# Edge sums of the first two layers of a four-layer graph network: partial sums gathered by PSUM strips of neighbouring node tiles

## The reference

```python
# layer 0 (attention, 4 heads)
h = x @ W;  e = leaky(a_src[src] + a_dst[dst]);  alpha = softmax of e over the edges of each dst
x1 = layernorm(x + prelu(segment_sum(alpha * h[src], dst) + bias))
# layer 1
msg = relu(x1[src] + edge_attr)
z = x1 + segment_sum(msg, dst);  then two dense layers and a norm
# layer 2: segment_sum(support[src] * edge_weight, dst)
# layer 3: attention over the edges with 8 heads, then a feed-forward part
```

## Time and profile before

| | us |
|---|---|
| median of the runs | 6502.33 |
| span of the profiled execution | 6898.0 |
| PE busy | 4580.7 (66%) |
| DVE busy | 4207.2 (61%) |
| ACT busy | 2924.2 (42%) |
| POOL busy | 4137.4 (60%) |

### The profile page before, as it was taken

The page is one execution under the profiler, slowest core; times in us unless marked ns, Lnnn a source line. Parts: engine busy times, 40 slices in busy tenths (PEclk is TensorE's granted clock), DMA queues, the critical chain, the costliest instruction groups (busy, mean ns, idle before and its releaser), DMA issues. The chain is left out here.

```text
span 6898.0 us, 99476 instructions
## 1 busy us (share of the span) xinstructions
PE 4580.7 (66%) x17620; PEld 3435.1 (50%) x17621; DVE 4207.2 (61%) x10350; ACT 2924.2 (42%) x8245; POOL 4137.4 (60%) x3730
## 2 busy tenths in 40 slices
PE   7366666660455555586777777775567777777799
PEld 5234344430233333375666666664455555555688
DVE  4366666677455555684444444445589988988554
ACT  0133233335233333252222222222278988888543
POOL 1666666632666666326888888883367777777110
PEclk9566666675676766797766777777888988988899
DMA  6344444424555555316888888886556656666110
GB/s 202 106 109 110 110 109 109 110 75 153 161 180 176 173 172 176 119 63 119 132 131 131 132 131 131 132 131 183 178 161 187 187 177 185 188 180 185 41 33 28
DMA packets 704342, 947.56 MB, mean 137 GB/s; under 512 B 99439, under 2 KB 560847, under 8 KB 704176
## 3 DMA queue, kind: packets, MB, share of 16 engines
q0 software_dynamic: 277808, 587.53, 37.0%
q1 hardware_dynamic: 406928, 338.53, 17.1%
q10 hardware_dynamic: 19440, 19.79, 0.8%
HBM read 756.06 MB, written 189.40 MB: 137 GB/s over the span
## 5 line engine op out<-in xcount | busy, mean ns | idle before, releaser
L1712 POOL DMA_INDIRECT gcn<-c_update,c_target x832 | 1300.0, 1563 | 271.5 <-issue 231.9
L1308 PE MATMUL psum<-g_rows,g_onehot 128*128 x1664 | 635.5, 532 | 745.8 <-issue 240.9
L664 POOL DMA_INDIRECT e_rows<-hrow,e_idx x832 | 822.3, 988 | 463.2 <-issue 236.9
L2078 POOL DMA_INDIRECT s_rows<-kv,s_idx x832 | 798.3, 960 | 372.0 <-issue 224.5
L1200 POOL DMA_INDIRECT g_rows<-x,g_idx x784 | 765.2, 976 | 414.7 <-issue 222.2
L1308 PEld LDWEIGHTS psum<-g_rows,g_onehot 128*128 128x128 f32 x1664 | 396.7, 260 | 984.5 <-issue 928.2
L727 PE MATMUL psum<-e_rows,e_onehot 128*128 128x265 f32 x1664 | 668.9, 559 | 275.0 <-issue 112.2
L2181 PE MATMUL psum<-queries_sums,s_spread 128*128 x1664 | 518.3, 466 | 249.4 <-issue 148.4
L727 PEld LDWEIGHTS psum<-e_rows,e_onehot 128*128 128x128 f32 x1664 | 403.6, 266 | 478.4 <-DVE acc L821 191.3
L1276 DVE TENSOR_TENSOR acc<-acc,psum 128x256 f32 x832 | 349.4, 420 | 439.6 <-issue 189.1
L1664 PE MATMUL psum<-support,c_mix 128*128 x1664 | 610.1, 531 | 0.0
(11 more groups left out here) (360 smaller groups left out, 9315.4 us busy)
## 6 DMA issues: line engine op xcount, KB each, us to landing
g_attr<-in_edge_attr SPq DMA_DIRECT2D x196, 512.0 KB
c_srow<-rows_src SPq DMA_DIRECT2D x208, 256.0 KB
e_drow<-rows_dloc SPq DMA_DIRECT2D x208, 128.0 KB
c_feat<-in_edge_feat SPq DMA_DIRECT2D x832, 32.0 KB
s_drow<-rows_dloc SPq DMA_DIRECT2D x208, 128.0 KB
n_sums<-gcn SPq DMA_DIRECT2D x100, 256.0 KB
e_rows<-hrow,e_idx POOLq DMA_INDIRECT x832
edge_rows<-c_edge_rows SPq DMA_DIRECT2D x208, 64.0 KB
```

Source lines behind the costliest of these rows:

```text
L664: pool.indirect_dma_start(rows[u][:, s, 0:D + H], None, k.hrow, bass.IndirectOffsetOnAxis(ap=idx[u][:, s:s + 1], axis=0)).then_inc(gathere ...
L1308: pe.matmul(k.psum[:, s, 0:D], onehot[q % 2][:, s, :], rows[:, bass.ds(m[q % 2 * GROUP + s], 1), :].rearrange("p o d -> p (o d)"), start=T ...
L1712: pool.indirect_dma_start(k.gcn[a], bass.IndirectOffsetOnAxis(ap=target[q][:, a:a + 1], axis=0), update[q][:, a, :], None, compute_op=ALU. ...
L2078: pool.indirect_dma_start(rows[at.u][:, st, 0:2 * D], None, k.kv, bass.IndirectOffsetOnAxis(ap=idx[at.u][:, st:st + 1], axis=0)).then_inc( ...
```

## The change

In each of the two layers the sums of several steps are gathered in PSUM before VectorE adds them.

*Layer 1.* A group has a strip of four neighbouring node tiles in PSUM (two banks; two strips take turns). The strip begins at the node tile of the group's first step (`base_at`, at most NT - 4); `part_at` holds for each step its place in the two strips. TensorE first writes zeros over the two banks (one-row bfloat16 matmuls of 512 columns), then adds the four steps into the places that the table names, and ends the two accumulations by two matmuls of 8 columns. VectorE adds the whole strip, 4 x 256 columns, in one instruction. TensorE waits once per group for the strip to be free (two groups back), POOL and `mark` count groups.

*Layer 0.* Two steps share a strip of two tiles, in two banks; two strips. The first step starts the first bank, a matmul of zeros starts the second, the second step goes to the bank that `second_part` names, and two matmuls of 8 columns end both. VectorE adds 2 x 265 columns per pair, and its order in a round is now: first pair of the group before, `weigh`, second pair, `mark`. TensorE reads two entries of `second_part` into registers per group.

Both layers get a few more small VectorE instructions ahead of their loops, to make the tables.

```diff
@@ gat_edges
-                        pool.wait_ge(summed, n * SB + (q + 1) * GROUP)
+                        pool.wait_ge(summed, n * PB + (q + 1) * 2)
...
             def add_up(n, u, q):
+                second = load_indices(nc, pe, second_part, n * PB + 2 * q, 2, 3)
                 pe.wait_ge(weighed, n * GB + q + 1)
                 pe.wait_ge(half_weighed, n * GB + q + 1)
                 pe.wait_ge(onehot_ready, n * GB + q + 1 + 1)
-                for s in range(GROUP):
-                    pe.wait_ge(added, n * NADD + q * GROUP + s + (3 if q else 1))
-                    pe.matmul(k.psum[:, s, 0:W], onehot[q % 2][:, s, :], rows[u][:, q * GROUP + s, :],
-                              start=True, stop=True).then_inc(summed, 1)
+                for h in range(2):
+                    pe.wait_ge(added, n * NADD + 2 * q + h + (3 if q else 1))
+                    here, beyond = 2 * h, 2 * h + 1
+                    pe.matmul(k.psum[:, beyond, 0:W], k.ones16[:], zero16[:], start=True, stop=False)
+                    pe.matmul(k.psum[:, here, 0:W], onehot[q % 2][:, 2 * h, :], rows[u][:, q * GROUP + 2 * h, :],
+                              start=True, stop=False)
+                    pe.matmul(k.psum[:, bass.ds(second[h], 1), 0:W].rearrange("p o w -> p (o w)"),
+                              onehot[q % 2][:, 2 * h + 1, :], rows[u][:, q * GROUP + 2 * h + 1, :],
+                              start=False, stop=False)
+                    pe.matmul(k.psum[:, here, 0:8], k.ones16[:], zero16[:, 0:8], start=False, stop=True)
+                    pe.matmul(k.psum[:, beyond, 0:8], k.ones16[:], zero16[:, 0:8], start=False, stop=True
+                              ).then_inc(summed, 1)
...
-            def add_group(n, q, js):
-                for s in range(GROUP):
-                    st = q * GROUP + s
-                    dve.wait_ge(summed, n * SB + st + 1 + 2 * SB)
-                    dve.wait_ge(added, n * NADD + 2 + st + GROUP)
-                    at = k.acc[:, bass.ds(js[st % 16], 1), :].rearrange("p o w -> p (o w)")
-                    dve.tensor_tensor(at, at, k.psum[:, s, 0:W], ALU.add).then_inc(added, 1)
+            def add_pair(n, q, h, js):
+                p = 2 * q + h
+                dve.wait_ge(summed, n * PB + p + 1 + 2 * PB)
+                dve.wait_ge(added, n * NADD + 2 + p + 2)
+                to = k.acc[:, bass.ds(js[p % 8], 2), :]
+                dve.tensor_tensor(to, to, k.psum[:, 2 * h:2 * h + 2, 0:W], ALU.add).then_inc(added, 1)
...
                         if not start:
-                            weigh(n - 1, 1 - u, q)
...
                             if q > 0:
-                                add_group(n - 1, q - 1, js)
+                                add_pair(n - 1, q - 1, 0, js)
+                            weigh(n - 1, 1 - u, q)
+                            if q > 0:
+                                add_pair(n - 1, q - 1, 1, js)
@@ gin_edges
+            by_group = lambda t: t[:].rearrange("o (g s) -> o g s", s=GROUP)
+            ch.tick(dve.memset(zero16[:], 0.0))
+            ch.then(dve.tensor_scalar(by_group(base_at), by_group(k.step_j)[:, :, 0:1].to_broadcast([1, GROUPS, GROUP]),
+                                      float(NT - GROUP), None, ALU.min))
+            ch.then(dve.tensor_tensor(part_at[:], k.step_j[:], base_at[:], ALU.subtract))
+            odd = part_at[:].rearrange("o (g b s) -> o g b s", b=2, s=GROUP)[:, :, 1, :]
+            dve.tensor_scalar(odd, odd, float(GROUP), None, ALU.add).then_inc(slots_ready, 1)
...
-            def step_group(at, j):
-                for s in range(GROUP):
-                    st = at.g * GROUP + s
-                    dve.wait_ge(summed, st + 1 + R)
-                    dve.wait_ge(stepped, st + GROUP)
-                    to = k.acc[:, bass.ds(j[s], 1), :].rearrange("p o w -> p (o w)")
-                    dve.tensor_tensor(to, to, k.psum[:, s, 0:D], ALU.add).then_inc(stepped, 1)
+            def sum_group(at, j):
+                dve.wait_ge(summed, at.g + 1 + 2)
+                dve.wait_ge(stepped, at.g + 2)
+                to = k.acc[:, bass.ds(j, GROUP), :]
+                dve.tensor_tensor(to, to, parts[:, at.q % 2 * GROUP:at.q % 2 * GROUP + GROUP, :], ALU.add
+                                  ).then_inc(stepped, 1)
...
+                        to = load_indices(nc, pe, part_at, at.g * GROUP, 2 * GROUP, 2 * GROUP - 1)
+                    pe.wait_ge(stepped, at.g + 1)
+                    banks = [k.psum[:, 2 * (q % 2) + n, :] for n in range(2)]
+                    for bank in banks:
+                        pe.matmul(bank, k.ones16[:], zero16[:], start=True, stop=False)
                     if at.has_tiles:
                         pe.wait_ge(msg_ready, at.g + 1 + RING)
                     pe.wait_ge(onehot_ready, at.g + 1 + 2)
                     for s in range(GROUP):
-                        pe.wait_ge(stepped, at.g * GROUP + s + 1)
-                        pe.matmul(k.psum[:, s, 0:D], onehot[q % 2][:, s, :],
-                                  rows[:, bass.ds(m[q % 2 * GROUP + s], 1), :].rearrange("p o d -> p (o d)"),
-                                  start=True, stop=True).then_inc(summed, 1)
+                        st = q % 2 * GROUP + s
+                        pe.matmul(parts[:, bass.ds(to[st], 1), :].rearrange("p o d -> p (o d)"), onehot[q % 2][:, s, :],
+                                  rows[:, bass.ds(m[st], 1), :].rearrange("p o d -> p (o d)"), start=False, stop=False)
+                    for bank in banks:
+                        ins = pe.matmul(bank[:, 0:8], k.ones16[:], zero16[:, 0:8], start=False, stop=True)
+                    ins.then_inc(summed, 1)
```

More of the change, by code:

```diff
@@ L588, in gat_edges @@
     T = SB + 1
-    NADD = SB + 2
+    PB = SB // 2
+    NADD = PB + 2
     SETUP = 5
@@ L614, in gat_edges @@
         scale = sb("e0_scale", [P, H])
+        first_tile, second_part = (sb(f"e0_{n}", [1, STEPS // 2], I32) for n in ("first_tile", "second_part"))
+        zero16 = sb("e0_zero16", [1, W], BF16)
         LOOK, WEIGHT, TURN, BACK = 4, 5, 6, 7
@@ L626, in gat_edges @@
                  "summed", "added", "chain", "cleared", "half_cleared"))
+        pairs_ready = sem("e0_pairs_ready")
         block = ctx.enter_context(nc.Block())
@@ L704, in _ @@
         def _(pe):
-            pe.sem_inc(summed, 2 * SB)
+            pe.wait_ge(pairs_ready, 4)
+            pe.sem_inc(summed, 2 * PB)
             pe.sem_inc(looked_up, 2)
@@ L770, in _ @@
             dve.sem_inc(spread_ready, RING)
-            dve.sem_inc(added, GROUP)
+            dve.sem_inc(added, 2)
             dve.sem_inc(onehot_ready, 1)
@@ L779, in _ @@
             assert setup.n == SETUP
+            of_pair = lambda a: k.step_j[:].rearrange("o (p a) -> o a p", a=2)[:, a, :]
+            dve.tensor_copy(first_tile[:], of_pair(0)).then_inc(pairs_ready, 1)
+            dve.tensor_tensor(second_part[:], of_pair(1), of_pair(0), ALU.subtract).then_inc(pairs_ready, 1)
+            dve.memset(zero16[:], 0.0).then_inc(pairs_ready, 1)
+            dve.wait_ge(pairs_ready, 3)
+            odd = second_part[:].rearrange("o (p a) -> o a p", a=2)[:, 1, :]
+            dve.tensor_scalar(odd, odd, 2.0, None, ALU.add).then_inc(pairs_ready, 1)
+            dve.wait_ge(pairs_ready, 4)
             dve.wait_ge(half_cleared, 1)
@@ L794, in mark @@
             def mark(n, q):
-                wait_if_any(dve, summed, n * SB + (q - 1) * GROUP + 2 * SB)
+                wait_if_any(dve, summed, n * PB + (q - 1) * 2 + 2 * PB)
                 one_hot(dve, k, onehot[q % 2], n * GB + q).then_inc(onehot_ready, 1)
@@ L808, in rescale @@
                 at = k.acc[:, bass.ds(j, 1), :].rearrange("p o w -> p (o w)")
-                dve.wait_ge(added, n * NADD + GROUP)
+                dve.wait_ge(added, n * NADD + 2)
                 dve.tensor_tensor(at[:, 0:D].rearrange("p (h c) -> p h c", h=H),
@@ L879, in _ @@
                         if not start:
-                            weigh(n - 1, 1 - u, q)
                             if q in (1, 5):
-                                js = block_steps(n - 1, q // 4)
+                                js = block_tiles(n - 1, q // 4)
                             if q == 1:
@@ L905, in _ @@
                         if q == GB - 1 and not start:
-                            add_group(n - 1, q, js)
+                            add_pair(n - 1, q, 0, js)
+                            add_pair(n - 1, q, 1, js)
                     assert ch.n == OPS, ch.n
@@ L909, in _ @@
             for q in range(GB):
-                weigh(last, 1, q)
                 if q in (1, 5):
-                    js = block_steps(last, q // 4)
+                    js = block_tiles(last, q // 4)
                 if q == 1:
@@ L915, in _ @@
                 if q > 0:
-                    add_group(last, q - 1, js)
+                    add_pair(last, q - 1, 0, js)
+                weigh(last, 1, q)
+                if q > 0:
```

(21 more changed lines are left out.)

7 lines of the change are left out of this document (3 added, 4 removed).

## The result

The changed kernel takes 6469.39 us (median of 4 runs, 6467.10 to 6472.59) where the kernel before takes 6504.03 in the same comparison: ratio 0.9949 [0.9935, 0.9963], 34.6 us less. The span of its profiled execution is 6469.9 us. So a comparison of those two profiles shows nothing of the change.

The account below looks back on a forecast made before the run. The prediction took POOL's gather issue, 1.26 us each, to bound layers 0 and 1 in timed runs; 0 in the gathering parts and -5 - 8 = -13 us at the ends took 6502 to 6489 us, own range 6465 to 6515.

Parts of the forecast that it names:

- Two of the signs it named: Span falls 150 to 300 us while the median moves under 30: then stalls were the profiled execution's own.
- Rivals 3: Layer 0 not at POOL's floor in timed runs; a quarter of its 214 us waits real: 6440 us, chance 0.13.
- here, 1: Stalls of VectorE's sequencer in layers 0 and 1 are in timed runs as well: 6260 us, chance 0.20.
- The stalls belong to the profiled execution: Layers 0 and 1: stalls absent or small in timed runs; 383 us of POOL's excess waits nearly match the 395.7 difference.
- my 230 us for them: Profiled execution only: 170 us of layer 1's waits and 60 of layer 0's 214 go, fewer sequencer rows.
- All of it lies beside POOL's 5.04 us: worth 0 there: VectorE, layer 1: group falls from 3.96 to 2.6 to 3.0 us, some 200 us, worth 0 while POOL gathers.
- Layer 0's gathers at 0: Layer 0's gathering part: VectorE's 5 us saved per block lies beside POOL's 40.3 us, so 0 in timed runs.
- Start of layer 0 at 0: Layer 0's four small table operations, some 2 us, lie under the first gathers and cost nothing.
- Layer 1's -5: Last 12 groups of layer 1, without gathers: 2.83 us each becomes 2.4, 5 us less.
- Layer 0's -8: Last two blocks' 16 rounds of layer 0, after the gathers: 0.65 us less each, taken as 8 us less.
- TensorE, layer 0: Added matmuls cost 0.5 us per pair, 8 per block: 30.5 becomes 38.5 of 40.3 us, the tightest place; expected to hold.
- rival 2: TensorE becomes layer 0's bound at 0.72 us per pair: 83 us slower, less the ends, 6575 us; chance 0.17.

Follow-up runs that it names:

- the reduction in front: Layer 1 changed alone, plus one VectorE reduction of 800 columns per group of layer 1 just ahead of the one-hot: 6487.76 us, ratio 0.9978 against the kernel before.

## Why the prediction was right and where it was wrong

The time, 6469, lies 20 us under the 6489 of the forecast and inside its own range (6465 to 6515), and the order of size was right: the stalls of the profile were not to be had in the timed comparison, and the rest is small. But the terms are others, and that the time fell into the range is luck: 34 of the 35 us come from the gathers of layer 1, which the sum has at 0 and no rival names. Two of the signs it named fail as well: the span fell by 428 us, not 150 to 300, and the median moved by 35 us, not by less than 30; the two spans are of different kinds. And layer 0 did not get shorter where profiles of one kind are compared: 1124.0 to 1128.7 us from first gather to last sum in four with the old layer 0, 1127.2 to 1133.9 in three with the strips, 1124.3 with the strips and `weigh` first.

- *Bounds.* POOL's floor of 1.26 us per gather sets layers 0 and 1: right, no wait of POOL in either once the stalls are away. But the floor itself was not reached: the gathers of layer 1 took 1023 us, not 988, and those of layer 0 1071, not 1048. Rivals 3 and, here, 1 fall.
- *Stalls.* "The stalls belong to the profiled execution" failed as it was put. They come in whole series, timed runs too. What held is that the 396 us between span and median belong to the stalls: span and time agree within 2 us as soon as both are of one series (6492.3 and 6494.16). Even where there are stalls, my 230 us for them were wrong: the parts gave -20 and +26, measured apart. The reason is above: the sum took the long sequencer steps for the cause, and the waits stayed when the steps were gone.
- *"All of it lies beside POOL's 5.04 us: worth 0 there"*, for VectorE in layer 1. This is the step that failed. It asked whether VectorE has time, not whether its instructions can hold POOL's. The term was -34.5 us between the two spans of gathers, by the moment of the one-hot: what the gathers behind a running one-hot took over the median fell from 36.7 to 1.9 us. The sign was on display: in the earlier trace rows the gather at 2858.35 takes 1.14 us, and 2857.98 + 0.68 + 0.83 = 2859.49 is its end.
- *Layer 0's gathers at 0.* Those held by the one-hot went from 60 (22.5 us) to 78 (24.8 us) with the strips, those held by the operation that writes `e_spread` from 4 to 25 (3.3 us), by the scan that writes `e_far` from 1 to 7 (2.7 us), while those held by the one that writes `e_links` fell from 24 (2.6 us) to 2. First to last gather came out 5.5 to 5.9 us longer against this one profile; over all profiles without stalls it is 1068.6 to 1073.2 us in four with the old layer 0 and 1073.6 to 1076.9 in four with the strips, so the term is smaller, some 4 us. The order around `weigh` is not what does it: with `weigh` first it is 1074.1.
- *Start of layer 0 at 0: "lie under the first gathers".* Failed: POOL's release hangs on TensorE's, and that now on the tables; POOL waits 4.70 us for it instead of 0.16.
- *The ends.* Layer 1's -5: from the last gather's start to the last sum 42.7 us before (2494.9 to 2537.6) and 40.0 after (2474.8 to 2514.8), -2.7. The group went from 2.83 to 2.51 us, not 2.4:

```profile
2510.06 0.20 PE L1351 MATMUL psum<-g_zero,ones 1*128 1x8 bf16 x2
...
2510.12 0.59 PE L1342 MATMUL psum<-g_zero,ones 1*128 1x512 bf16 x2
...
2510.64 1.99 PE L1348 MATMUL psum<-g_rows,g_onehot 128*128 x8
...
2512.57 0.20 PE L1351 MATMUL psum<-g_zero,ones 1*128 1x8 bf16 x2
```

  Layer 0's -8 did not come: 53.2 us before (1263.3 to 1316.5), 49.6, 55.7 and 56.0 in three profiles with the strips (last gather's start to L741's last).
- *TensorE, layer 0.* Taken as 8 us per block; 125.6 us more in 900 are 5.7 per block of 41 us. The clock fell, 0.76 to 0.73, where I expected it to rise from 0.65. That it holds was right, and that it is the tightest place is shown by the 219 us of two more matmuls: rival 2 was less than two such matmuls per pair away.
- *Prices.* The 1024-column addition 1.22 us as said. The zeros as records, means over both clock levels:

```profile
L1342 PE MATMUL psum<-g_zero,ones 1*128 1x512 bf16 x416 | 147.9, 441 | 166.7 <-issue 166.7
L734 PE MATMUL psum<-e_zero,ones 1*128 1x265 bf16 x416 | 136.0, 327 | 97.0 <-DVE e_rows L826 77.2 <-DVE acc L842 15.1 <-ACT e_rows L680 2.2
L740 PE MATMUL psum<-e_zero,ones 1*128 1x8 bf16 x416 | 74.2, 178 | 0.0
```

The sum by the two profiles without stalls (6492.3, and 6462.9 of the changed kernel's second): start +5.6 (4.5 of it the wait), layer 0's gathers +5.5, its end -3.6 (+2.5 and +2.8 in the other two profiles), layer 1's gathers -33.8 (1023.2 to 989.4), its end -2.4, the rest -0.7; together -29.4.

## What to carry to other kernels

Where POOL issues DMAs back to back, look at the durations of its own instructions, not only at its idle time: a mean well above the median (here 1002 against 953 ns) can be a hold by VectorE, and here it depended on the moment, not the amount, of VectorE's work. Take one input of such an operation out of SBUF, or move it to where no gather starts. The layer 1 strips gained by accident what `iota` in PSUM gains on purpose, and layer 0's strips cost a little (8 us alone, nothing measurable beside layer 1's) and are better left out. Before terms are summed, profile and times must be of the same kind of run; and a strange duration beside a lost time is not yet its cause.

`iota` in PSUM without strips (6456.99, 0.9933) beats the kernel before clearly and stands level with the changed kernel (0.9945) within the intervals; it was not tried together with layer 1's strips.

## What the runs showed of the hardware

- A gather started while the one-hot runs (680 ns, both inputs in SBUF) ends 0.83 us after that operation; free, it takes 0.95 us. So the hold costs up to 0.5 us, and nothing if no more than 0.12 us of the operation are left. If the one-hot starts less than 0.04 us ahead of the gather, the gather is free and the one-hot takes 0.05 to 0.08 us longer (six cases in the kernel before, 25 with the reduction in front).
- With one of the two inputs in PSUM the same operation (0.68 us either way) holds nothing: none of 134 gathers. Other operations with an input in PSUM hold nothing either: none of 595.
- Two inputs in SBUF are not the only case: the operation that writes the bfloat16 `e_spread`, with one tensor as input, held 25 gathers of layer 0 (3.3 us) in the changed kernel.
- In one whole series of runs, timed and profiled, this kernel took 6% longer, with VectorE standing still for up to 11 us (and once 25 us) before an addition. Sequencer steps of 0.7 to 1.4 us came with it where VectorE had many of them, but the lost time was there without them too. That series ran on one chip of the machine and the three later ones, without stalls, on three others; whether it is the chip or something else stays open.
